# Message passing over 212,500 edges: seven pairs of eight with a tile made of columns, written-out programs, positions loaded by fours

## What is computed

```
msg_in     = concat([x[src], x[dst], edge], -1)           # 64 + 64 + 32
messages   = relu(msg_in @ mW1 + mb1) @ mW2 + mb2         # hidden 128
aggregated = segment_sum(messages, dst, n)
out        = relu(concat([x, aggregated], -1) @ uW1 + ub1) @ uW2 + ub2
return layernorm(x + out)
```

## Time and profile before

| | |
|---|---|
| median of 3 runs | 1921.3 us (1914.27 to 1922.36) |
| the profiled execution | 1922.22 us |
| its span | 1920.4 us |
| granted TensorE clock, mean | 0.804 of full speed |
| busy: TensorE, its weight loads, VectorE, ScalarE, GpSimd | 1429.3, 1334.2, 1540.8, 1242.0, 1431.4 us |
| gathers from `table_src` (L717) | 1465 |
| copies of a column (L469), ScalarE and VectorE | 9428 and 9408 |

### The profile page before, as it was taken

The page is one execution under the profiler, slowest core; times in us unless marked ns, Lnnn a source line. Parts: engine busy times, 40 slices in busy tenths (PEclk is TensorE's granted clock), DMA queues, the critical chain, the costliest instruction groups (busy, mean ns, idle before and its releaser), DMA issues.

```text
span 1920.4 us, 56413 instructions
## 1 busy us (share of the span) xinstructions
PE 1429.3 (74%) x8716; PEld 1334.2 (69%) x8716; DVE 1540.8 (80%) x10793; ACT 1242.0 (65%) x10165; POOL 1431.4 (75%) x1527
## 2 busy tenths in 40 slices
PE   6776677777678777767768777776867878777877
PEld 6776566777667677666667667766767767766776
DVE  5568888888888888888888888888888888888883
ACT  3246766767766766766666666766666666766663
POOL 7777777777777777777777777777777777777773
PEclk8898888778877878788887887878788776877686
DMA  9664444444444444444444444444444444444441
GB/s 239 163 154 113 123 114 114 123 115 114 123 113 114 124 115 112 120 118 113 115 123 113 112 122 117 114 119 120 112 115 123 113 114 122 115 114 119 118 109 35
DMA packets 169379, 229.86 MB, mean 120 GB/s; under 512 B 98508, under 2 KB 117687, under 8 KB 168701
## 3 DMA queue, kind: packets, MB, share of 16 engines
q1 hardware_dynamic: 112484, 124.14, 23.4%
q0 software_dynamic: 48416, 97.68, 20.6%
q10 hardware_dynamic: 8254, 5.59, 1.2%
HBM read 217.59 MB, written 9.60 MB: 118 GB/s over the span
## 4 chain that ended last, share of the span: by engine, by line
POOL 63%; issue 23%; PE 4%; DVE 3%; DMA 3%; DVEq 1%; ACT 1%; POOLq 1%; SPq 1%; ACTq 0%
POOL gath L717 63%; DVE col_x L469 2%; DMA gath<-table_src,idx 1%; PE ps_sum L856 1%; DVEq L460 1%; DMA table_src<-gath 1%; PE ps_pre L824 1%; PE ps_pre L825 1%; DVE hid L1180 1%; PE ps_pre L790 0%; PE ps_pre L832 0%; POOLq L302 0%; DMA xwin<-in_xT_dram 0%; ACT hid L1000 0%; DMA col_src<-in_srcT_dram 0%
## 5 line engine op out<-in xcount | busy, mean ns | idle before, releaser
L717 POOL DMA_INDIRECT gath<-table_src,idx x1388 | 1309.6, 944 | 423.0 <-issue 420.6
L469 ACT COPY col_x<-xdeg 64x1 f32 x9428 | 912.4, 187 | 237.6 <-issue 219.6
L832 PE MATMUL ps_pre<-rhs,lhs 128*128 128x128 f32 x3226 | 603.0, 363 | 448.3 <-DVE lhs L1158 445.6
L469 DVE COPY col_x<-xdeg 64x1 f32 x9408 | 718.2, 138 | 216.0 <-issue 215.5
L832 PEld LDWEIGHTS ps_pre<-rhs,lhs 128*128 128x128 f32 x3226 | 558.8, 269 | 477.1 <-DVE lhs L1158 473.9
L856 PE MATMUL ps_sum<-onehot,hid 128*128 128x96 f32 x3322 | 473.2, 304 | 13.0 <-ACT rhs L976 11.9
L856 PEld LDWEIGHTS ps_sum<-onehot,hid 128*128 128x128 f32 x3322 | 463.3, 221 | 23.5 <-issue 15.2
L1007 ACT ACTIVATE hid<-hid 128x1024 f32<-128x1024 f32 x202 | 212.5, 1052 | 180.4 <-DVE hid L1180 177.0
L1180 DVE TENSOR_TENSOR hid<-ps_pre,gath 128x1024 f32<-128x1024 f32 x202 | 246.4, 1220 | 87.2 <-DMA gath<-table_src,idx 75.4
L1158 DVE TENSOR_SCALAR_CACHE_REDUCE lhs<-lhs,place 96x1024 f32<-96x1024 int32 x208 | 264.6, 1272 | 32.7 <-PE ps_sum L765 19.8
L1150 DVE TENSOR_TENSOR onehot<-ps_iota,dst_rel 128x768 f32<-128x768 f32 (+1 forms) x209 | 196.9, 943 | 0.1
(11 more groups left out here) (109 smaller groups left out, 639.1 us busy)
## 6 DMA issues: line engine op xcount, KB each, us to landing
lhs<-in_dst_dram SPq DMA_DIRECT2D x207, 384.0 KB
lhs<-in_edgeT_dram SPq DMA_DIRECT2D x207, 128.0 KB
gath<-table_src,idx POOLq DMA_INDIRECT x1388
table_src<-gath SPq DMA_DIRECT2D x12, 512.0 KB, 7.0
xwin<-in_xT_dram SPq DMA_DIRECT2D x208, 24.0 KB
idx<-in_srcT_dram SPq DMA_DIRECT2D x192, 4.0 KB
out_dram<-yout ACTq DMA_DIRECT2D x48, 64.0 KB, 1.6
col_src<-in_srcT_dram SPq DMA_DIRECT2D x148, 0.5 KB
```

The source lines that it names most:

```text
L469: ins = copy(col_x[:, i, start + n + j:start + n + j + 1], col)
L717: pool.indirect_dma_start(gath[0:m, k, j * H:(j + 1) * H], None, table_src, src_by_tile(p, k, j, m)).then_inc(gathered[k], 16)
L832: mm = nc.tensor.matmul(to[0:m, j * H:(j + 1) * H], lhs[:, k, j * P:j * P + m], rhs[:, k, :], start=True, stop=not by_cols)
```

## The change

- Every pair from 13 on whose number isn't a multiple of eight has the tile made of columns (`has_cols`): 171 pairs with the last, where it was 147.
- A tile's 64 copies on an engine are now two batches of 32 (`COL_BATCH`). In step p, ScalarE and VectorE make the second batch for pair p + 1 and then the first for pair p + 2. ScalarE loads the registers of a second batch already behind the first (`act_regs`). `col_src` and `col_x` have four slots, and there is one pair of counters, `cols_act` and `cols_dve`.
- A pair with all tiles gathered (16, 24, ...) puts its eighth into `gath_x`, and VectorE adds it by an instruction of its own, since that tile of `gath` stays zero for all slots.
- The positions of `add_sums` are loaded by fours in steps k = 3 (`load_starts`), without a bound check.
- The programs of all engines are written out; `pairs` has no loop left.

```diff
+EARLY = 16
+COL_FROM = 13
+COL_SKIP = 8
+COL_BATCH = COL_HALF // 2
-COL_PLAN = (((2, 0, 32), (1, 48, 16)), ((2, 32, 32), (0, 0, 16)), ((0, 16, 32), (0, 48, 16)), ((1, 0, 32), (1, 32, 16)))
...
-            if looped:
-                with eng.Fori(LAG, ITERS - 1) as it:
-                    both(it, it - LAG)
+            for it in range(ITERS - 1):
                 for k in range(SLOTS):
                     step(it, k)
+                    if it >= LAG:
+                        for stage in STAGES[k]:
+                            node(it - LAG, stage, NP)
...
+        def has_cols(p):
+            return COL_FROM <= p < PAIRS and p % COL_SKIP != 0
...
+        def load_regs(eng, k, start, count):
             regs = [eng.alloc_register(f"col{next(col_regs)}") for n in range(count)]
-            eng.load(regs, col_src[0:1, i, start:start + count])
+            eng.load(regs, col_src[0:1, k, start:start + count])
+            return regs
...
+        def wait_cols(eng, p):
+            k = p % SLOTS
+            eng.wait_ge(col_src_in[k], col_loads(p))
+            if col_before(p) is not None:
+                eng.wait_ge(pe_steps, steps_for_pre(col_before(p)))
+            let(eng)
...
# SyncE
+                p = it * SLOTS + k + PREP
+                if has_cols(p):
+                    load_cols(p, col_tile(p), P, col_before(p), col_src_in[p % SLOTS])
...
# GpSimd
-                for j, m in tiles_of(p):
-                    if j == rows_of(p) or j == COL_TILE and has_cols(it, k):
-                        break
-                    pool.indirect_dma_start(gath[0:m, k, j * H:(j + 1) * H], None, table_src, src_by_tile(p, k, j, m)).then_inc(gathered[k], 16)
+                for j, m in tiles_of(p)[0:gathers_of(p)]:
+                    to = gath_x[:, :] if p > COL_FROM and j == COL_TILE else gath[0:m, k, j * H:(j + 1) * H]
+                    pool.indirect_dma_start(to, None, table_src, src_by_tile(p, k, j, m)).then_inc(gathered[k], 16)
...
# ScalarE, step, behind relu
-                copy_cols(act, nc.scalar.copy, it, k, 0, 0, cols_act)
-                copy_cols(act, nc.scalar.copy, it, k, 1, 0, cols_act)
+                p = it * SLOTS + k
+                if has_cols(p + 1):
+                    copy_batch(act, nc.scalar.copy, (k + 1) % SLOTS, COL_BATCH, act_regs.pop(), cols_act)
+                if has_cols(p + 2):
+                    to = (k + 2) % SLOTS
+                    wait_cols(act, p + 2)
+                    copy_batch(act, nc.scalar.copy, to, 0, load_regs(act, to, 0, COL_BATCH), cols_act)
+                    act_regs.append(load_regs(act, to, COL_BATCH, COL_BATCH))
...
# VectorE
+                spare = p > COL_FROM and not has_cols(p)
+                at = slice(0, (COL_TILE if spare else rows_of(p)) * H)
+                ins = nc.vector.tensor_tensor(hid[:, k, at], ps_pre[k % 2][:, at], gath[:, k, at], ALU.add)
+                if spare:
+                    at = slice(COL_TILE * H, PW)
+                    ins = nc.vector.tensor_tensor(hid[:, k, at], ps_pre[k % 2][:, at], gath_x[:, :], ALU.add)
+                ins.then_inc(hsum_made, 1)
...
+            def load_starts(p):
+                regs = [dve.alloc_register(f"start{p + i}") for i in range(SLOTS)]
+                dve.load(regs, start_i[0:1, p:p + SLOTS])
+                starts.update((p + i, reg) for i, reg in enumerate(regs))
...
-                    start = dve.value_load(start_i[0:1, cols(p, 1)], min_val=0, max_val=WMAX)
-                at = bass.ds(start, WIN)
+                at = bass.ds(dve.snap(starts.pop(p), donate=True, min_val=0, max_val=WMAX), WIN)
...
-                copy_cols(dve, nc.vector.tensor_copy, it, k, 0, COL_HALF, cols_dve)
+                if p % SLOTS == SLOTS - 1:
+                    load_starts(p - SLOTS + 1)
+                if has_cols(p + 1):
+                    to = (k + 1) % SLOTS
+                    copy_batch(dve, nc.vector.tensor_copy, to, COL_HALF + COL_BATCH, load_regs(dve, to, COL_HALF + COL_BATCH, COL_BATCH), cols_dve)
...
-                copy_cols(dve, nc.vector.tensor_copy, it, k, 1, COL_HALF, cols_dve)
+                if has_cols(p + 2):
+                    to = (k + 2) % SLOTS
+                    wait_cols(dve, p + 2)
+                    copy_batch(dve, nc.vector.tensor_copy, to, COL_HALF, load_regs(dve, to, COL_HALF, COL_BATCH), cols_dve)
```

More of the change, by code:

```diff
@@ L357, in steps_for_window, with pairs @@
             return p - 2
-        def pairs(eng, step, node, tail, peeled=PEELED, looped=True):
-            for it in range(peeled if looped else LAG):
+        def pairs(eng, step, node, tail):
+            for it in range(ITERS - 1):
                 for k in range(SLOTS):
                     step(it, k)
-            if looped:
[L366 to L376, removed]
-                with eng.Fori(LAG, ITERS - 1) as it:
-                    both(it, it - LAG)
-            else:
-                for it in range(LAG, ITERS - 1):
-                    both(it, it - LAG)
+                    if it >= LAG:
+                        for stage in STAGES[k]:
+                            node(it - LAG, stage, NP)
             def end(i, stage):
@@ L386, in end @@
                 node(c, stage, NP if c < CHUNKS else LAST, i)
-            both(ITERS - 1, ITERS - 1 - LAG)
+            for k in range(SLOTS):
+                step(ITERS - 1, k)
+                for stage in STAGES[k]:
+                    node(ITERS - 1 - LAG, stage, NP)
             end(0, UPD)
@@ L415, in raw @@
             return hid[:, r, j * D:(j + 1) * D] if r < SLOTS else raw_x[:, r - SLOTS, j, :]
[L417 to L427, removed]
@@ L562, in load_idx @@
             def load_idx(p, it, k):
-                if not (isinstance(p, int) and p < (PEELED + 1) * SLOTS):
+                if p >= EARLY + SLOTS:
                     sp.wait_ge(hsum_made, p - SLOTS + 1)
@@ L829, in pre @@
                 for j, m in tiles_of(p):
-                    last = [i for i, tile, count in LAST_COLS if is_last(p) and tile == j]
-                    by_cols = last or j == COL_TILE and has_cols(it, k)
+                    by_cols = has_cols(p) and (j == col_tile(p) or j == TILES and is_last(p))
                     mm = nc.tensor.matmul(to[0:m, j * H:(j + 1) * H], lhs[:, k, j * P:j * P + m], rhs[:, k, :], start=True,
@@ L915, in _ @@
                 pe.wait_ge(rows_out[0], len(TABLE))
-                pairs(pe, step, node, tail, looped=False)
+                pairs(pe, step, node, tail)
             with pe.Else():
@@ L1252, in _ @@
             with dve.If(fit == 1):
-                pairs(dve, step, node, tail, looped=False)
+                pairs(dve, step, node, tail)
             with dve.Else():
```

158 lines of the change are left out of this document (62 added, 96 removed).

## The result

The changed kernel is **slower**: 2060.3 us median of 4 runs (2057.8 to 2062.2) against 1921.2 us of the kernel before beside it, a ratio of 1.073 (1.070 to 1.076). The profiled execution has a span of 2058.4 us, where it was 1920.4: 138 us more.

What follows compares the result with a forecast made beforehand. GpSimd's gathers bounded the kernel before; VectorE, paced by its issuing queue, would become the bound. 142 us start, 193 steps of 9.54 us (1841), 33 us tail and 1.8 us beyond the span gave 2018 us; range 1953 to 2062 us.

Steps and rivals of the forecast that it cites:

- rival 2: ScalarE becomes the bound, with two loads of 32 and 64 copies: 9.75 us a pair, 2059 us; chance 0.15.
- The gathers: On GpSimd: 24 gathers less, 30 us of slack; waits for VectorE's addition 0.6 us a pair, some 130 us.
- A full step: VectorE, six steps of eight, each with two batches of 32 copies: 10.06 us.
- The step of pair 6: VectorE's step with only its first batch, second part bare arithmetic: 6.5 us.
- The load of four positions: VectorE's register load in pair 3's step, not hidden once in eight pairs: 0.5 us.
- The start: Addition of pair 12 on VectorE, where the long stretch begins: about 142 us, against some 148 before.
- the tail: What follows the long stretch, the last pairs' chain through TensorE, left unchanged: 33 us.
- The step of pair 7: VectorE's step with only its second batch, first part all arithmetic: 7.4 us before output chunk and TensorE wait.
- With 0.7 us: VectorE's wait for TensorE in the short steps, once in eight pairs, taken from 0.2 to 1.5 us.
- I cost it at nothing: ScalarE: full step 9.6 us, under VectorE's 10.06, node work fitting the two short steps; no time added.
- Rivals 1, 3 and 4: VectorE's low end, 1953 us, chance 0.12; GpSimd stays bound, 1892 us, 0.07; a draw, 1915 to 1930 us, 0.02.
- code loading: Gaps of 0.22 us inside VectorE's runs of copies; 0.05 us added to a full step for more instructions.

Runs made afterwards that it cites:

- the run with fixed columns: The changed kernel with VectorE's first batch of 32 copying fixed columns, without register loads: 1949.1 us, one run.
- the fours: The kernel before with the positions loaded by fours and nothing else, still looped: 3019.0 us against 3027.1, ratio 0.998.
- three of four: The changed kernel with column tiles in three pairs of four (COL_SKIP = 4): 3192.7 us (ratio 1.044) and 3158.0 us (ratio 1.043).
- the long sets: Sets of runs on two of the four chips, where every kernel took over half as long again; the kernel before took 3057 and 3027 us.
- five tiles of six: Against the kernel before: five tiles of six by columns, batches spread evenly, positions by fours, written out: 1899.3 us, ratio 0.989.

## Why the prediction came out as it did

**The mechanism held.** VectorE's issuing queue took the place of GpSimd, and 24 gathers less were worth nothing. The size is less good than the range makes it look: 2060.3 us is 42 above the likeliest and 2 under the upper end, and the range reached so far only to take in rival 2, whose mechanism isn't what happened. With its own upper value for the wait on TensorE, 1.5 us, the forecast's sum gives 77.2 us for eight pairs and 2039 us. That the measured time lies inside is luck; what bears the forecast out is the chain and the steps. Point by point:

- *The gathers.* GpSimd waits 147 us in its long stretch; forecast was some 130 of 0.6 us a pair. The waits name the load of the indices for 127 us of this and VectorE's addition for only 11, where the forecast named the addition; that this load is late because the pairs are is my reading and wasn't tried.
- *A full step*, 10.06 forecast: the five with nothing else are 10.21, 10.15, 10.13, 10.22 and 10.12 us in the mean, 0.5 us more in all. From the compare to the batch it is 2.83 us. The registers' price held: 2.10 us for 32. The Trainium skill's figure ("Runtime: NRT & Kernel Launch", section "Instruction fetch mechanics": about 200 ns for each register) would make that load 6.4 us; the trace does not agree. The same page of the Trainium skill, section "Terms", has such loads come from HBM; here the source is SBUF, and no run loads from HBM. The preference for written-out code in the first of these sections gained nothing either: ratio 0.999.
- *The step of pair 6*, 6.5 forecast, is 6.49.
- *The load of four positions*, 0.5 forecast, takes 0.346 us in 52 loads; pair 3's step, forecast 10.96 with the output chunk, is 10.85.
- *The start*, 142 us forecast, was 142.7; the tail, 33 us forecast, was 28.7.
- *The step of pair 7* is **the term that was mis-sized**. The prediction had 7.4 us, with the output chunk's 0.4 and "With 0.7 us" for the wait on TensorE: 8.5. It is 9.99 us. All but 0.05 of the difference is that wait, 2.2 us instead of 0.7.

The sum by eight pairs is 78.15 us where 76.4 was forecast: 1.5 us from the step of pair 7, 0.5 from the full steps, 0.2 less elsewhere. Over the 193 steps that is 1887 us instead of 1841; with a start 0.7 us later and a tail 4.3 us shorter the forecast's span of 2016 becomes the measured 2058.4.

Why the wait was taken too small: I had TensorE's time from the start of the tile products to the end of the window product as anything from 2.9 to 4.2 us, from two steps, and took a wait below the middle. In the steps of pair 6 it is 4.46 us in the mean, above even the upper end, and the wait is 1.27 (compare) + 0.15 + 4.46 + 0.13 - 3.87 = 2.1 us. The prediction had "0.2 to 1.5 us": its upper end lacked the two spaces around TensorE's work, 0.3 us together, and 0.26 us of the work.

The two rows were the ends of a spread, and the trace of before could have told which end is common: of 189 steps of its long stretch the sixteen tile products take over 3.2 us in 90 and under 2.4 us in 47. In the changed kernel it is 112 and 29, and of the 23 steps of pair 6 that its trace has whole none is under 2.5 us. The slow kind was the commoner one before the change already, and the change made it more common. Beside the two kinds shown stands a different clock: from 783.7 to 787.3 us the granted clock is 0.53, and from 790.0 to 791.9 us, behind work without a gap, it is 1.00, close to the two levels of 1.2 and 2.4 GHz. What lowers it isn't shown. The rows above and the earlier trace rows suggest idle TensorE ahead of the products (3.42 us behind 4.59 us of idle time, 2.05 behind 1.40), but it is no rule for a single step: ahead of the products of pair 6 TensorE is idle for 0 to 3.0 us, and they are slow behind work without a gap as well:

```profile
706.02 0.64 PE L832 MATMUL ps_sum<-ident,deg 96*128 96x96 f32 x2
706.44 3.02 PE L810 MATMUL ps_pre<-rhs,lhs 128*128 128x128 f32 x16
```

**The rivals.** ScalarE as the bound (rival 2) has nearly the measured number, 2059 us, by another mechanism; in the changed kernel's chain ScalarE has 2%, and in the run with fixed columns it makes the same copies at 9.2 us a pair, so it isn't what sets 9.78. It was closer than "I cost it at nothing" sounds: a full step of ScalarE, 9.6 us by the prediction, is 9.4 to 10.3 us from 1001 to 1041 us of that run, where the chain goes through ScalarE, and TensorE's wait for its window copy (L950) is 68.4 us in the changed kernel. Rivals 1, 3 and 4 fall with the 9.78 us a pair.

What stays open: how much the fours and three of four are worth on a chip without that disturbance, since their runs fell into the long sets; what lowers TensorE's clock here; and what the changed kernel would take if only the wait of the pair 7 step were gone, which no run tried by itself.

## To carry to other kernels

Spread work that an issuing queue bounds over all the places where arithmetic can cover it, before counting how much of it there is: the same copies cost 2060 us in 14 half steps of 16 and 1947 us in 16 of 16. Move work from the bound engine only as far as the next engine's need, here five tiles of six, and read that need from the stretch where the bound one is still ahead. When a duration has a slow and a quick value in the trace, don't take a middle from two rows: count both over the whole stretch, and price a wait by the commoner one, here the slow.

## What was not expected of the hardware

- Registers are loaded on VectorE in 0.31 us for one, 0.346 for four, 1.10 for 16, 2.10 for 32: from four on some 0.063 us for each further one. Loading four at once is nearly free beside one.
- A 64-element copy costs VectorE's path 0.075 us with its address in a register (2.41 us for 32) and 0.063 with a fixed one (2.02 us for 32). Where the queue is ahead of the engine, register-addressed ones too take 0.063 (32 in 2.02 us in the time line of the positions by fours), so the difference lies in the queue.
- The gaps of 0.2 to 0.3 us inside runs of copies are tied to places in the program: in the traces of before and after, 92 and 110 of them, each stands 128 of VectorE's instructions, or a multiple of that, behind the one ahead (to within one). Together they are 24 and 29 us. This fits the prediction's reading as code loading, which no run varied.
- In two sets of runs the medians of all kernels were 3019 to 3193 us. The trace of the kernel before written out shows how, in VectorE's time line:

```profile
1010.74 0.21 DVE L469 COPY col_x<-xdeg 64x1 f32 x2 [1.20 <-issue]
1012.18 0.20 DVE L469 COPY col_x<-xdeg 64x1 f32 x2 [1.24 <-issue]
1013.61 0.21 DVE L469 COPY col_x<-xdeg 64x1 f32 x2 [1.23 <-issue]
1015.04 0.21 DVE L469 COPY col_x<-xdeg 64x1 f32 x2 [1.22 <-issue]
```

Copies that otherwise follow each other every 0.075 us come in pairs with 1.2 us between, and ScalarE's likewise (1338 us of "issue" ahead of its copies, where it is 214 in the trace of the same kernel in the usual set). The looped kernel before was as slow (3057 and 3027 us), so it isn't the unrolled code. Its cause wasn't found.
